# State-space phase of a four-layer model: the product with C written over the states, state buffers 2 to 4, and a new spacing of the background pieces

## The reference, cut to what matters

```python
def step(h, inp):
    u_t, d_t, B_t, C_t = inp
    dA = jnp.exp(d_t[..., None] * A)
    h = h * dA + (d_t * u_t)[..., None] * B_t[:, :, None, :]
    y = jnp.einsum('bkdn,bkn->bkd', h, C_t)
    return (h, y)
...
xn = _layernorm(xi, ln1_g, ln1_b)
xz = xn @ in_proj_w.T
xc, z = jnp.split(xz, 2, axis=-1)
xc = xc.transpose(0, 3, 1, 2)
xc = jax.lax.conv_general_dilated(xc, conv_w, (1, 1), 'SAME', feature_group_count=DI) + conv_b[None, :, None, None]
xc = jax.nn.silu(xc)
...
delta = jax.nn.softplus(jnp.einsum('bkrl,kdr->bkdl', dts, dt_w) + dt_b[None, :, :, None])
...
y = _layernorm(y, outn_g, outn_b)
y = y * jax.nn.silu(z)
out = xi + y @ out_proj_w.T
```

## Time and profile before

| | us |
|---|---|
| median of 3 runs | 11986.81 |
| lowest, highest | 11973.92, 11987.67 |
| profiled execution, its own time | 12019.25 |
| its span | 12017.4 |
| first scan to the end of the last step of `layer0` | 119.3 to 4799.7 |

### The profile page before, as it was taken

The page is one execution under the profiler, slowest core; times in us unless marked ns, Lnnn a source line. Parts: engine busy times, 40 slices in busy tenths (PEclk is TensorE's granted clock), DMA queues, the critical chain, the costliest instruction groups (busy, mean ns, idle before and its releaser), DMA issues. The chain is left out here.

```text
span 12017.4 us, 158137 instructions
## 1 busy us (share of the span) xinstructions
PE 9655.9 (80%) x57482; PEld 5113.2 (43%) x57482; DVE 7526.3 (63%) x7471; ACT 5899.4 (49%) x11044; POOL 5634.9 (47%) x4841
## 2 busy tenths in 40 slices
PE   7777877787778777455469999999999999789997
PEld 2322332233223223344445555555555555433334
DVE  5789977997899999344445554544555553344532
ACT  4555555555555555111126666666666665333233
POOL 5778877886788887455633323222232221011010
PEclk9999999999999999787889999999999999899988
DMA  1112221221122222555420000000000000300003
GB/s 67 61 66 73 78 66 60 70 79 63 61 71 79 71 72 68 155 151 150 140 77 1 5 1 5 1 5 4 1 5 1 5 1 17 115 1 1 1 1 130
DMA packets 259800, 624.10 MB, mean 52 GB/s; under 512 B 26759, under 2 KB 115183, under 8 KB 256728
## 3 DMA queue, kind: packets, MB, share of 16 engines
q1 hardware_dynamic: 204696, 439.59, 11.1%
q0 software_dynamic: 51840, 169.91, 4.8%
q10 hardware_dynamic: 2496, 4.49, 0.1%
HBM read 572.72 MB, written 40.90 MB: 51 GB/s over the span
## 5 line engine op out<-in xcount | busy, mean ns | idle before, releaser
L723 DVE TENSOR_TENSOR_SCAN a_H<-a_pA,a_dBu 128x962 f32<-128x962 f32 (+1 forms) x1280 | 2661.1, 2079 | 184.8 <-DVE a_hC L732 43.5
L937 POOL TENSOR_TENSOR a_dBu<-a_du,a_Bs 128x960 f32<-128x960 f32 (+1 forms) x1280 | 2742.5, 2143 | 0.1
L873 ACT ACTIVATE a_pA<-a_delta,a_al 128x480 f32<-128x480 f32 (+1 forms) x2560 | 1626.0, 638 | 1643.9 <-DVE a_H L723 1643.3
L515 PE MATMUL a_pY<-a_hC,cst 128*128 128x480 f32 (+1 forms) x5120 | 2244.0, 561 | 71.0 <-ACT a_Y L890 71.0
L732 DVE TENSOR_TENSOR a_hC<-a_H,a_pC 128x960 f32<-128x960 f32 (+1 forms) x1280 | 1395.3, 1090 | 124.7 <-PE a_pC L515 124.2
L515 PEld LDWEIGHTS a_pY<-a_hC,cst 128*128 128x128 f32 x5120 | 987.8, 195 | 727.7 <-issue 546.3
L515 PE MATMUL a_pC<-a_stk,a_sel 96*128 96x480 bf16 (+1 forms) x1280 | 476.7, 372 | 845.8 <-DVE a_hC L732 842.1
L1041 POOL DMA_INDIRECT b_gath<-b_tab,b_idx x648 | 727.0, 1122 | 548.9 <-PE b_pS L1092 318.5
L1092 PE MATMUL b_pS<-cst,b_gath 128*128 128x128 f32 x2592 | 432.7, 346 | 583.5 <-DVE b_gath L1170 555.1
L2357 POOL TENSOR_TENSOR c_KF<-c_KF,c_dg 128x1056 f32<-128x1056 f32 x192 | 385.0, 2006 | 1046.7 <-DVE c_MX L2126 1045.5
L3282 POOL TENSOR_TENSOR e_P<-e_P 128x1024 f32<-128x1024 f32 (+1 forms) x80 | 151.8, 1919 | 1475.1 <-ACT e_P L3258 1475.1
(11 more groups left out here) (453 smaller groups left out, 17867.3 us busy)
## 6 DMA issues: line engine op xcount, KB each, us to landing
a_Bs<-a_brows SPq DMA_DIRECT2D x512, 480.0 KB
a_Bs<-a_brows SPq DMA_DIRECT2D x128, 384.0 KB
d_W<-in_d_w SPq DMA_DIRECT2D x32, 1024.0 KB, 7.5
f_W<-in_f_w SPq DMA_DIRECT2D x32, 1024.0 KB, 7.5
b_tab<-b_TT SPq DMA_DIRECT2D x32, 576.0 KB
b_gath<-b_tab,b_idx POOLq DMA_INDIRECT x648
a_zt<-a_sz SPq DMA_DIRECT2D x36, 256.0 KB
a_sz<-a_zt SPq DMA_DIRECT2D x16, 480.0 KB, 4.9
```

The lines of the kernel that those rows point to most:

```text
L515: return pe.matmul(out, lhsT, rhs, start=start, stop=stop, skip_group_check=True)
L723: v.tensor_tensor_scan(span(H[:, g % 2, :], g), factors(g), span(dBu[:, g % ND, :], g), 0.0, ALU.mult, ALU.add).then_inc(S(kind), 1)
L873: s.activation(pA[:, k, at:at + z], delta[:, u % 2, h, 0:z], ACT.Exp, scale=al[:, o + 2 * d, h, n:n + 1]).then_inc(S(kind), 1)
L937: g.tensor_tensor(inner(dBu[:, i % ND, :], i), du[:, u % 2, :, 0:z], Bs[:, p % NB, i % 2, 0:z].unsqueeze(1).broadcast_to([128, 2, z]), ALU ...
```

## The change

- a_hC is gone. `hc` writes its product over the states in a_H, which now has four buffers (NH = 4); the four take 3848 elements of a partition where the two and two took 3844. `hc` g therefore has to wait for `carry` g (ACT copies the end states first), and `add` g reads a_H.
- Scan g waits for `add` g-4 in place of `hc` g-2 and `carry` g-2. `hc` no longer waits for `add`.
- SiLU gets an empty step ahead of si_inv and ahead of si_out; both layer norms get one ahead of their norm; the softplus gets one ahead of sp_max, and du is put with sp_max, with no steps behind.
- The halves of a map of the front run one after the other (`one_by_one`), each holding one bank; only the maps ahead of the first scan still use `both`.
- The drain of `proj` is at n = 12, behind the step's own `next`. In the first five units of images 1 to 3 every fourth step takes two further pieces.

```diff
-    H = ph.sb("H", [128, 2, 2 * CS + 2])
-    hC = ph.sb("hC", [128, 2, 2, CS])
+    H = ph.sb("H", [128, NH, 2 * CS + 2])
...
+    def one_by_one(*jobs):
+        for job in jobs:
+            yield from job
...
         ph.put("si_min", what, b, h, c)
         yield
+        yield
         ph.put("si_inv", what, b, h, c)
+        yield
         yield
         ph.put("si_out", what, b, h, c)
...
-    def norm(b, c):
+    def norm(b, c, halves=one_by_one):
...
         yield
+        yield
         ph.put("f_norm", b, c)
         give(("f_centre", (b, c)), ("f_norm", 5 * b + c + 1))
         yield
-        yield from both(front_in(b, 0, c), front_in(b, 1, c))
+        yield from halves(front_in(b, 0, c), front_in(b, 1, c))
...
-    def convs(b, c):
-        yield from both(conv(b, 0, c), conv(b, 1, c))
+    def convs(b, c, halves=one_by_one):
+        yield from halves(conv(b, 0, c), conv(b, 1, c))
...
             ph.put("sp_ln", u, h)
             yield
+            yield
             ph.put("sp_max", u, h)
             give(("dt", (u, h)), ("sp_max", k + 1))
-            yield
             ph.put("du", u, h)
-            yield
...
-        while n == N - AHEAD - 2 and next(nxt, "end") != "end":
+        next(nxt, None)
+        while n == N - AHEAD - 1 and next(nxt, "end") != "end":
             further()
-        next(nxt, None)
-        for _ in range(2 if u < 4 else 1):
+        for _ in range(2 if u < 4 or UB <= u and u % UB < 5 and n % 4 == 3 else 1):
             further()
...
-                        m = mm(pY[:, h, 0:size(g)], ident, hC[:, g % 2, h, 0:size(g)], n == 0, n == N - 1)
+                        m = mm(pY[:, h, 0:size(g)], ident, inner(H[:, g % NH, :], g)[:, h, :], n == 0, n == N - 1)
...
-                    if g >= 2:
-                        v.wait_ge(S("carry"), g - 1)
-                        v.wait_ge(S("hc"), g - 1)
-                    v.tensor_tensor_scan(span(H[:, g % 2, :], g), factors(g), span(dBu[:, g % ND, :], g),
+                    if g >= NH:
+                        v.wait_ge(S("add"), g - NH + 1)
+                    v.tensor_tensor_scan(span(H[:, g % NH, :], g), factors(g), span(dBu[:, g % ND, :], g),
                                          0.0, ALU.mult, ALU.add).then_inc(S(kind), 1)
...
-                    if g >= 2:
-                        v.wait_ge(S("add"), g - 1)
+                    v.wait_ge(S("carry"), g + 1)
                     v.wait_ge(S("scan"), g + 1)
-                    v.tensor_tensor(hC[:, g % 2, :, 0:z], inner(H[:, g % 2, :], g),
+                    v.tensor_tensor(inner(H[:, g % NH, :], g), inner(H[:, g % NH, :], g),
                                     pC[:, 0:z].unsqueeze(1).broadcast_to([128, 2, z]), ALU.mult).then_inc(S(kind), 1)
```

More of the change, by code:

```diff
@@ L148, in layer0 @@
     fb = ph.sb("fb", [105, CS])
-    NB, ND, AHEAD = 3, 4, 3
+    NB, ND, NH, AHEAD = 3, 4, 4, 3
     Bs = ph.sb("Bs", [128, NB, 2, CS])
     dBu = ph.sb("dBu", [128, ND, 2 * CS + 2])
-    H = ph.sb("H", [128, 2, 2 * CS + 2])
-    hC = ph.sb("hC", [128, 2, 2, CS])
+    H = ph.sb("H", [128, NH, 2 * CS + 2])
     sq = ph.sb("sq", [128, 2, BP])
@@ L287, in norm, with gate @@
         yield
-        yield from both(front_in(b, 0, c), front_in(b, 1, c))
-    def gate(b, c):
-        yield from both(front_z(b, 0, c), front_z(b, 1, c))
+        yield from halves(front_in(b, 0, c), front_in(b, 1, c))
+    def gate(b, c, halves=one_by_one):
+        yield from halves(front_z(b, 0, c), front_z(b, 1, c))
         ph.put("z_store", b, c)
-    def convs(b, c):
-        yield from both(conv(b, 0, c), conv(b, 1, c))
+    def convs(b, c, halves=one_by_one):
+        yield from halves(conv(b, 0, c), conv(b, 1, c))
     def front(b, first=0):
@@ L363, in first_maps @@
     def first_maps():
-        yield from norm(0, 0)
-        yield from both(norm(0, 1), gate(0, 0))
-        yield from both(convs(0, 0), gate(0, 1))
+        yield from norm(0, 0, both)
+        yield from both(norm(0, 1, both), gate(0, 0, both))
+        yield from both(convs(0, 0, both), gate(0, 1, both))
         yield from proj(0)
@@ L880, in _ @@
                         s.wait_ge(S("joined"), g + 1)
-                    s.activation(carry[:, :, n], edge(H[:, g % 2, :], g, True), ACT.Copy).then_inc(S(kind), 1)
+                    s.activation(carry[:, :, n], edge(H[:, g % NH, :], g, True), ACT.Copy).then_inc(S(kind), 1)
                 elif kind == "y_out":
```

## The result

The changed kernel takes 11682.71 us in the median of four runs (11680.43 to 11688.44), the one before 11986.54 (11973.92 to 11987.67). The ratio is 0.975, interval 0.9733 to 0.9766: 304 us or 2.5% faster. Forecast were 11625 us, 362 us less; the measured gain is 58 us short of it. The profiled execution of before lay 32 us above its median, that of after took 11683.06 us, so part of the 336 us between the two profiles is that execution's, and lies in the later layers (7193.5 us from their first VectorE instruction to the end before, 7165.8 after). In `layer0` the scans start from 119.3 to 4796.3 us before and from 119.9 to 4484.9 after: 4677.0 and 4365.0 us from the first to the last start, 312 less.

What follows compares the result with a forecast made beforehand. VectorE (DVE) was taken to bound a quiet step, with 437 us of the phase lost to background work. Gap 164 and stops 198 (437 less 239 put back) made 362 us off 11987: 11625 us, range 11520 to 11780.

Steps and rivals of the forecast that it cites:

- the case of the forecast: Whole kernel: a gain of 270 to 480 us, that is 11505 to 11715 us; chance 0.75.
- The gap closes: Scan directly behind a product on VectorE: starts 1.05 us after the product's start, not 1.26; 780 places, 164 us gained.
- New waits cost nothing: Product's wait for `carry`, scan's wait for `add` g-4 and the in-place product: cost 0.
- Rival 3: In-place product on VectorE is dearer: at 0.4 us more each it costs 512 us, 12137 us; chance 0.03.
- nothing in that wait is late: Scan g's wait for `add` g-4: PE did that `add` long before, so the wait holds nothing up.
- The stops go: Drain bursts at n = 11 vanish: 437 us lost to background work, 239 put back for spread pieces, 198 us gained.
- Convolution: Three convolution steps in a row on PE outlast VectorE: 2.8 us for each of 32 triples, 90 us put back.
- Units 0 and 1, 2 and 3: Bursts in units 0 and 1, some 19 us standstill each, and three-piece steps in units 0 to 3: 50 us put back.
- VectorE pieces and ACT: 161 background pieces on VectorE, 56 us, and front pieces meeting y_out or px copies on ACT, 35 us, put back.
- The end: Behind the last scan: three output pieces in place of two, 8 us put back.
- what the profile was to show: Signs: quiet units 52 to 53 us, a_pC waits 60 to 130 us, scans' idle time a fraction of 184.8 us.

Runs made afterwards that it cites:

- buffers only: The kernel before with the change's four state buffers, in-place product and waits, but its own order of background pieces: 11842.02 us, ratio 0.9885.
- order only: The changed kernel with the two state buffers, two product buffers and waits of before, its order of pieces kept: 11822.71 us, ratio 0.9864.
- the wait put back: The changed kernel with one wait more, scan g waiting again for product g-2 directly ahead of it: 11827.32 us, ratio 0.9866.
- without empty steps: The changed kernel without the empty steps in SiLU and the two layer norms, that of the softplus kept: 11686.87 us, ratio 0.9706.
- row reads: The changed kernel with px and inject reading the map row by row in all units (other places' values): 11661.27 us, ratio 0.9691.

## Why the prediction was right, and where it was short

The range (11520 to 11780) held 11683, and the case of the forecast (gain 270 to 480) is the one that came. By its steps:

- *The gap closes.* Forecast 164 us; measured 139 in the loop (before against buffers only), 148 (order only against changed) and 149 (the wait put back). The mechanism is shown by the last, at the place itself: 1.04, 1.27. The size was 15 us too large. In the quiet stretch the pace gained 0.11 us a step (3.315 to 3.205), half of what one place gains. Step by step, the changed kernel against the wait put back: the forecast took the steps with px as unchanged, but the 39 steps n = 1 that prepare a column-wise unit became longer, by 12.7 us together. Such a step held 4.17 us in the earlier trace rows and holds 3773.99 - 3769.39 = 4.60 us now:

```profile
3769.39 2.15 DVE L728 TENSOR_TENSOR_SCAN a_H<-a_pA,a_dBu 128x962 f32<-128x962 f32 x1
...
3771.64 0.56 ACT L817 ACTIVATE a_stk<-a_pM 32x480 bf16<-32x480 f32 x1 [2.40 <-PE a_pM L521]
...
3772.56 1.22 ACT L877 ACTIVATE a_pA<-a_delta,a_al 128x480 f32<-128x480 f32 x2
...
3773.99 2.16 DVE L728 TENSOR_TENSOR_SCAN a_H<-a_pA,a_dBu 128x962 f32<-128x962 f32 x1 [0.98 <-POOL a_dBu L941]
```

ScalarE waits 2.40 us for px before it can copy it, and the exponentials of the next scan stand behind its copies. (The profile names POOL's a_dBu as what ended the scan's wait. That is a product for a later scan, which ended at the same moment; the one that this scan takes was over at 3765.79.) The forecast also missed `inject` in column-wise units: with 3.38 us on PE it holds the step at n = 10 at 3.5 us in the quiet units of after, and these 40 steps gained 1.5 us in place of 40 x 0.21 = 8.4.
- The rule of the Trainium skill that this term is 0 ("VectorE: DVE Perf Modes", section "The DRAIN you can't avoid") does not describe this pair: with the wait 1.27 us start to start, without it 1.04, with nothing but that wait between the two kernels. The measurement that the section gives is of eight copies in a row, and the section adds that a next operation that is not held starts earlier, without a figure. I had read only half of it.
- *New waits cost nothing.* Nearly right: VectorE has no wait for `carry`, and the product kept its 1091 ns. Rival 3 is out. But "nothing in that wait is late" does not hold for the wait for `add` g-4: the scan waited for it 33 times, 16.5 us together and 1.4 at most, most often at n = 3 (19 times), shortly behind the first `add` of a unit, which waits for y_out. What this adds to the time was not separated.
- *The stops go.* Forecast 198 us with the 8 of the end taken off, so 206 in the loop; measured 164 there (order only). This is the term that was most in error. Why they go was argued as the bank that is free for the preparation. The runs bear that out as the largest part (160 of 197 without empty steps), not as the only one.
- *Convolution.* 90 us put back; measured 88, 2.7 us a triple against 2.8. That the number fits is in part luck: by the forecast's picture spaced pieces would have fitted beside DVE, and spacing them gave back 31 us only. The 88 is what two thirds of the convolution's matmuls cost in this kernel; that the cost lies in their standing in three steps running is not shown.
- *Units 0 and 1, 2 and 3.* 50 us put back. They take 256.9 us (119.9 to 376.8) where the first four of the quiet stretch take 211.8 (3713.6 to 3925.4): 45. The stop of 19 us a burst shows as 21.1 us between two scans, so 18 more than a step.
- *VectorE pieces and ACT.* 56 + 35 us put back. This is what was too small. In the kernel with the order alone 4512.7 + 3.4 - 4243 = 273 us are lost to background work from the first scan to the last step; less the 88 and the 45, both taken from the changed kernel, an estimated 140 are left, against 91. The stretches of five output units take 271.3 and 273.1 us where five quiet ones take 256.4, 15 to 17 us more each (I had some 6 a stretch for VectorE's 18 pieces). The waits of the scan for ACT's exponentials are 92.5 us in 109 places, where before had 3.1 for them and 15.0 for `carry`; with the row reads they are 56.9, so part of them comes from px. What each piece is worth was not separated.
- *The end.* 8 us, measured 3.0: one output piece more stands behind the last scan, but the first of them starts earlier.
- Two slips in the bounds change nothing: ACT at its lower bound gives 35 us, not 30, and a gain of 270 to 480 from 11987 is 11507 to 11717 us.
- Of what the profile was to show: a quiet unit with a full chunk takes 53.0 us (211.8 / 4) where 55 stood, front stretches are within 8%, the clock rose, a_XC's waits are under 40 us, no wait of over 5 us from unit 2 on. Two points failed: the waits for a_pC are 155 us, not 60 to 130, and the scans' idle time is 127.6 us, not a fraction of 184.8.

In sum the loss against the forecast is 15 us of gap and 42 of order, less 5 at the end: 52 of the 58, and the rest is within what medians of these runs differ by. The column-wise reads, which cost 76 us in the changed kernel, are in no term of the forecast except as two steps a unit taken off the gap: a shorter step uncovered work of PE that the longer one had hidden.

## What to carry over

When an in-order engine alternates two instructions, look from start to start: an instruction that waits for its direct neighbour can lose a fifth of a microsecond at each place, and one more buffer removes that. Background pieces that share buffers with the preparation of the next round should hold as few as they can, or the drain at the deadline turns into a burst; read the bursts from the order, their price from the trace. And when the step gets shorter, go through every piece on the other engines again at the new length; the ones that just fitted are the next bound.

## What the runs showed of the hardware

Matmuls of 480 columns of float32 whose moving operand steps by 48 elements took 3.38 us for four instructions, the same ones read contiguously 1.77 us. A scan of 962 elements behind a product of 960 started 0.08 us before the shown end of that product if it did not wait for it (3795.74 + 1.12 against 3796.78), and 0.13 to 0.14 us behind it if it did (3859.03 + 1.13 against 3860.30); with 768 elements the wait cost 0.16 us from start to start, with 960 it cost 0.22.
